# Turning x1 and the experts' rows with 32x32 transposes on VectorE instead of 128x128 products on TensorE

## The reference

```python
x = x + cond_linear(x, cond, w0)            # x1: (4, 1024, 512) fp32, 4096 tokens
# cond_linear: ys = y/sqrt(512); d = rsqrt((ys*ys) @ (w*w) + 1e-8); ((x*ys) @ w) * d
shared = silu(xf @ w1) * (xf @ w3) @ w2     # 512 -> 1024 -> 512, xf = x1 by rows
s = sigmoid(concat([xf, cond]) @ router_W)  # 8 experts; the top 2 of s + bias are used
gates = s_sel / (s_sel.sum + 1e-9)          # combine[token, expert]
h = gelu(einsum('nc,ech->enh', xf, W1e)); y = einsum('enh,ehc->enc', h, W2e)
out = x1 + (shared + sum_e combine * y) / 3 # experts 512 -> 512 -> 512
```

## Time and profile before

| | before |
|---|---|
| time, median of 3 runs | 1152.32 us (1144.98 to 1153.76) |
| the profiled execution's own time | 1147.5 us |
| its span | 1145.7 us |
| PE busy | 1115.5 us, 97% of the span |
| PEld, DVE, ACT, POOL busy | 923.1, 416.6, 334.3, 252.1 us |
| DMA | 218.19 MB, mean 190 GB/s |
| granted TensorE clock | 0.995 of full speed |

### The profile page before, as it was taken

One profiled execution on the slowest core, in us unless ns is written; L12 is line 12 of the kernel. 1 busy time (PEld: TensorE's weight loads), 2 busy tenths in 40 slices (PEclk: granted clock), 3 DMA queues, 4 the chain that ended last, 5 costly groups with the idle time before them and its releaser, 6 DMA issues.

```text
span 1145.7 us, 15826 instructions
## 1 busy us (share of the span) xinstructions
PE 1115.5 (97%) x5260; PEld 923.1 (81%) x5261; DVE 416.6 (36%) x654; ACT 334.3 (29%) x552; POOL 252.1 (22%) x285
## 2 busy tenths in 40 slices
PE   7999999999999999999999989999998899999996
PEld 6888888888888888888887878888887788888884
DVE  6554345657332242323222133333332233333332
ACT  4443533232312122222111123333332222333321
POOL 0000000001121545556620001222211222222222
PEclk9999999999999999999999999999999999999999
DMA  4666867666746897887683088645487854454442
GB/s 168 234 246 255 302 248 257 213 244 240 250 146 230 274 303 276 296 289 223 183 220 110 5 291 284 154 83 98 84 260 250 270 88 85 82 101 81 74 80 40
DMA packets 74141, 218.19 MB, mean 190 GB/s; under 512 B 16176, under 2 KB 17328, under 8 KB 62832
## 3 DMA queue, kind: packets, MB, share of 16 engines
q1 hardware_dynamic: 38240, 133.83, 33.4%
q0 software_dynamic: 21856, 56.72, 22.2%
q10 hardware_dynamic: 14016, 27.27, 7.3%
HBM read 119.40 MB, written 98.65 MB: 190 GB/s over the span
## 4 chain that ended last, share of the span: by engine, by line
PE 59%; DMA 29%; POOL 4%; issue 3%; DVE 2%; SPq 1%; ACT 1%; POOLq 0%; ACTq 0%; DVEq 0%
DMA xs_d<-xrow,sadr 13%; PE banks L489 10%; PE banks L491 10%; PE banks L490 10%; DMA xs_d<-xrow,padr 7%; DMA we<-we_d 5%; PE banks L418 3%; PE banks L417 3%; PE banks L416 3%; PE banks L392 3%; PE banks L379 3%; PE banks L381 3%; PE banks L380 3%; PE banks L475 2%; PE banks L482 2%
## 5 line engine op out<-in xcount | busy, mean ns | idle before, releaser
L1085 POOL DMA_INDIRECT out<-ys,slot x71 | 110.2, 1552 | 448.2 <-DMA out<-ys,slot 266.9
L416 PE MATMUL banks<-xh,w13h 128*128 128x512 f32 x512 | 199.5, 390 | 0.9 <-issue 0.9
L417 PE MATMUL banks<-xl,w13h 128*128 128x512 f32 x512 | 199.2, 389 | 0.0
L418 PE MATMUL banks<-xh,w13l 128*128 128x512 f32 x512 | 199.2, 389 | 0.0
L781 DVE TENSOR_TENSOR gm<-sil,banks 128x512 f32<-128x512 f32 x64 | 43.9, 686 | 273.3 <-ACT sil L603 273.3
L603 ACT ACTIVATE sil<-banks 128x512 f32<-128x512 f32 x64 | 38.2, 597 | 336.8 <-PE banks L418 336.8
L489 PE MATMUL banks<-we,hidth 128*128 x284 | 118.9, 419 | 7.3 <-SPq L312 4.1
L489 PE MATMUL banks<-we,xgth 128*128 x284 | 119.0, 419 | 3.6 <-issue 3.3
L416 PEld LDWEIGHTS banks<-xh,w13h 128*128 128x128 f32 x512 | 96.1, 188 | 21.2 <-issue 1.1
L1002 DVE TENSOR_TENSOR xgtl<-banks,xgth 128x512 fp32r<-128x512 f32 x71 | 49.0, 691 | 174.7 <-ACT xgth L665 174.7
L417 PEld LDWEIGHTS banks<-xl,w13h 128*128 128x128 f32 x512 | 96.1, 188 | 19.9
(11 more groups left out here) (156 smaller groups left out, 1582.3 us busy)
## 6 DMA issues: line engine op xcount, KB each, us to landing
we_d<-ehl SPq DMA_DIRECT2D x32, 1024.0 KB, 4.8
we<-we_d SPq DMA_DIRECT2D x16, 2048.0 KB, 9.0
xg<-xs_d ACTq DMA_DIRECT2D x36, 512.0 KB, 4.4
eraw<-expert_w SPq DMA_DIRECT2D x32, 512.0 KB, 4.4
xrow<-x_d POOLq DMA_DIRECT2D x64, 256.0 KB, 3.4
xin<-xT SPq DMA_DIRECT2D x8, 1024.0 KB, 6.6
x1t_d<-x1t SPq DMA_DIRECT2D x8, 1024.0 KB, 8.7
x_d<-x1tok ACTq DMA_DIRECT2D x8, 1024.0 KB, 8.9
```

The source lines that it names most:

```text
L416: pe.matmul(ps[hc % 2][:, :], w_hi, xh[:, j, c, :], start=(c == 0), stop=False)
L417: pe.matmul(ps[hc % 2][:, :], w_hi, xl[:, j, c, :], start=False, stop=False)
L418: last = pe.matmul(ps[hc % 2][:, :], w_lo, xh[:, j, c, :], start=False, stop=(c == DC - 1))
L1085: pool.indirect_dma_start(out[:, :], IO(slot[:, t, 0:1], 0), ys[:, t % RING, :], None, compute_op=ALU.add).then_inc(added, 16)
```

## The change

- by_token and `idrw` go. `logits(n)` makes 16 fp32 products a block in its place: the stationary side is 32 columns of router weights (`rwide`), the moving side a 128x128 piece of x1t, and the four token pieces s write to partitions 32s to 32s + 31 of `log_ps`. VectorE turns the logits at the end by two 128x512 transposes.
- VectorE turns x1 itself, by 32x32 blocks: four transposes a block (`turn_x1`), from `xin` in the shared stage, steps 4 and 5 of the block before (block 0 after its own step 0). SP stores the result in four transfers of 32 partitions with runs of 512 bytes (`store_x1`, after step 5), into an `x1_d` whose columns are in another order and whose 128-row tiles hold tokens in another order (`token_ids`). `x1tok` shares memory with `outst`, so turns and outputs wait for each other's stores.
- POOL no longer waits for all of x1: `load_row` waits block by block on `x1_out`. It loads each tile once (32 loads) and scatters it twice, in pairs of tiles; ScalarE's waits before block 7 stay. SP's wait for the scatters and the load of `slot` are moved behind the stores and loads of blocks 5 to 7.
- transpose_x goes. The sorted rows come in by four transfers of 32 partitions with 512-byte runs (`load_rows`) for each pair of tiles, and VectorE turns them by one transpose a tile (`turn_x`).
- The factor 1/3 moves from `output` into `product`.

```diff
-        x1tok = sb("x1tok", [2, SUB, D], FP32, 160)
+        xgt = sb("xgt", [2, DC, P], FP32, 192)
+        x1tok = sb("x1tok", [BLK // Q, DC, Q], FP32, 168)
...
+            def store_x1(n):
+
+                sp.wait_ge(x1_turned, DC * (n + 1))
+                for g in range(P // Q):
+                    sp.dma_start(x1_d[n * BLK:(n + 1) * BLK, g * P:(g + 1) * P].rearrange("(a t) d -> t a d", t=Q),
+                                 x1tok[g * Q:(g + 1) * Q].rearrange("p a c n -> p a (c n)")).then_inc(x1_out, 16)
...
             for n in (NBLK - 2, NBLK - 1):
                 store_out(n - 1)
                 load_res(n)
+                if n < NBLK - 1:
+                    store_x1(n + 1)
             weight_loaded(0)
+            sp.wait_ge(pad_out, 16 * 2 * E)
+            for b in range(XB):
+                sp.wait_ge(xrow_out[b], 16 * (K * NT // XB))
+            sp.dma_start(slot[:, :, :], xs_rec).then_inc(slots_in, 16)
...
-                for s in range(SUB):
-                    pe.wait_ge(x1_done, 4 * n + s + 1)
-                    for o in range(DC):
-                        last = pe.matmul(tok_ps[s % 2][:, o // 2, o % 2 * (P + E):(o % 2 + 1) * (P + E)],
-                                         x1t[:, j, o, s * P:(s + 1) * P], idrw[:, o, :], start=True, stop=True)
-                    last.then_inc(tok_done, 1)
+            def logits(n, j):
+
+                for o in range(DC):
+                    pe.wait_ge(x1t_done, 4 * n + o + 1 + 2)
+                    for s in range(SUB):
+                        last = pe.matmul(log_ps[s * Q:(s + 1) * Q, n // 4, n % 4 * P:(n % 4 + 1) * P], rwide[:, o * E:o * E + Q],
+                                         x1t[:, j, o, s * P:(s + 1) * P], start=(o == 0), stop=(o == DC - 1))
+                last.then_inc(log_done, 1)
...
                 for k in range(1, RING + 1):
                     t = RING * i + k
                     matmul1(t, k)
-                    transpose_x(t + 1, k + 1, i + (k + 1) // RING)
                     matmul2(t - 1, k - 1)
                     transpose_h(t, k)
...
-                act.dma_start(xg[:, k % RING:k % RING + PAIR, :],
-                              xs_d[bass.ds(t * P, PAIR * P), 0:D].rearrange("(t p) d -> p t d", p=P)).then_inc(xg_in[j], 16)
+                for g in range(P // Q):
+                    act.dma_start(xg[g * Q:(g + 1) * Q, k % RING:k % RING + PAIR].rearrange("p t a n -> p (t a) n"),
+                                  xs_d[bass.ds(t * P, PAIR * P), g * P:(g + 1) * P].rearrange("(a r) d -> r a d", r=Q)).then_inc(xg_in[j], 16)
...
+            def turn_x1(n, j, c):
+
+                if c == 0:
+                    if isinstance(n, int) and n < 2:
+                        if n:
+                            dve.wait_ge(x1_out, 16 * (P // Q) * n)
+                    else:
+                        dve.wait_ge(out_stored, 16 * (n - 1))
+                dve.transpose(x1tok[:, :, c, :], xin[:, j, c, :].rearrange("p (a t) -> p a t", t=Q)).then_inc(x1_turned, 1)
...
+                if more and hc in (4, 5):
+                    turn_x1(n + 1, (j + 1) % 2, 2 * hc - 8)
+                    turn_x1(n + 1, (j + 1) % 2, 2 * hc - 7)
...
+            def turn_x(t, k, turn):
+
+                if k % PAIR == 0:
+                    dve.wait_ge(xg_in[k // PAIR % 2], 16 * (P // Q) * (turn + 1))
+                dve.transpose(xgt[:, k % 2].rearrange("p c (a r) -> p a c r", r=Q),
+                              xg[:, k % RING].rearrange("p a (c n) -> p a c n", n=Q)).then_inc(xturn_done, 1)
...
+            def load_row(i):
+
+                n, a = i // SUB, i % SUB
+                if a == 0:
+                    pool.wait_ge(x1_out, 16 * (P // Q) * (n + 1))
+                pool.dma_start(xrow[:, i % XB, 0:D],
+                               x1_d[n * BLK:(n + 1) * BLK, :].rearrange("(s a t) d -> a s t d", a=SUB, t=Q)[a]).then_inc(xrow_in[i % XB], 16)
...
+            for i in range(0, NT, 2):
+                for k in range(K):
+                    put_row(i, k)
+                    put_row(i + 1, k)
+                for m in (i, i + 1):
+                    if m + XB < NT:
+                        row_free(m)
+                        load_row(m + XB)
```

More of the change, by code:

```diff
@@ L35 @@
 PADROWS = P
+Q = 32
 ROW = D + 2
@@ L188, in shared_moe_kernel @@
         tok_done = sem("tok_done")
-        x1_done = sem("x1_done")
+        log_done = sem("log_done")
         x1t_out = [sem(f"x1t_out{j}") for j in range(2)]
-        x1_out = [sem(f"x1_out{j}") for j in range(2)]
+        x1_turned, x1_out = sem("x1_turned"), sem("x1_out")
         w_high, w_split = sem("w_high"), sem("w_split")
@@ L468, in _ @@
                     shared_block(2 * h + j, j)
-            def transpose_x(t, k, turn):
-                if k % PAIR == 0:
-                    pe.wait_ge(xg_in[k // PAIR % 2], 16 * turn + 16)
-                pe.wait_ge(xgt_done, t + 1)
-                for c in range(DC):
-                    last = pe.transpose(xt_ps[k % 2][:, c * P:(c + 1) * P], xg[:, k % RING, c * P:(c + 1) * P], ident)
-                last.then_inc(tx_done, 1)
             def transpose_h(t, k):
@@ L955, in _ @@
                 block_step(0, hc, 0, True)
+                if hc == 0:
+                    for c in range(DC):
+                        turn_x1(0, 0, c)
                 if hc in (0, 2, 4):
@@ L1063, in _ @@
             pool.dma_start(xrow[:, XB - 1, D:ROW].bitcast(INT32), padslots[:, 0:2]).then_inc(zero_in, 16)
-            for q in range(XB - 1):
-                load_row(q)
+            for i in range(XB - 1):
+                load_row(i)
             pool.wait_ge(zero_in, 32)
```

126 lines of the change are left out of this document (54 added, 72 removed).

## The result

| | before | after |
|---|---|---|
| time, median (runs) | 1154.3 us (20) | 1159.89 us (20), 1148.28 to 1171.11 |
| ratio to the kernel before, 95% interval | | 1.0062 (1.0032 to 1.0092) |
| the profiled execution's own time | 1147.5 us | 1156.24 us |
| its span | 1145.7 us | 1154.4 us |
| granted TensorE clock | 0.995 | 0.977 |

What follows compares the result with a forecast made beforehand. PE was taken to bound the shared stage, POOL's chain of adding scatters the experts' stage up to scatter 57. 1147.5 - 17 + 20 + 1 = 1151.5, plus 4.8 for the median: 1156 us, range 1138 to 1178.

Steps and rivals of the forecast that it cites:

- Logits, -17 us: Linear stage to up(0,0): narrow products run side by side, 1.3 us a group, less two x1t waits of 2.2 us; -17 us.
- VectorE's turns, 0: Shared stage: VectorE's 32 turns of x1, 22 us of work, hide beside PE and cost nothing.
- x1's store and the scatters, +20: Around block 7: x1's late store delays POOL's last scatters, ScalarE waits, PE stalls; +20 us (+16 to +30).
- it would reach this load some 35 us before x1 is there: POOL's chain reaches its load of tile 28 early and waits some 35 us for block 7 of x1.
- L: Time from a scatter's issue to its landing in POOL's chain to xs_d: 3.2 us (2.8 to 4.5).
- 5.0 + 2L: POOL's time for a pair of tiles scattered to xs_d in two waves, before it loads the next.
- Experts' stage, +1: PE saves 31 us in 71 tiles, but POOL's scatter chain is the bound; +1 us (-18 to +29).
- the +9 for 512-byte runs: Experts' stage: short-run row loads slow 56 quiet scatters by 0.16 us each, to 5.9 us; +9 us.
- Serial products: Rival: the narrow logits products run one after the other, -3 in place of -17; 1170 us, chance 0.25.
- Slower scatters: Rival: 512-byte runs make the experts' stage scatters 6.3 us or more, +22; 1178 us, chance 0.12.
- The faster case: Rival: scatters less disturbed, 5.4 us each, about -20, 1136 us; or block 7's stall goes; chance 0.2.
- The 5.4 for an undisturbed scatter: Experts' stage: the last scatter, 3.81 + 1.55 us, read as the time of a scatter without loads beside it.

Runs made afterwards that it cites:

- experiment 4: Changed kernel with the two loops of the logits exchanged, so four products in a row write to the same 32 partitions: 1172.45 us, ratio 1.0162.
- f1: Changed kernel, but POOL's loads bring 128 neighbouring rows of x1_d instead of four stretches of 32 rows: 1150.42 us, ratio 0.9977.
- f3: Changed kernel with the 64 loads and the load and scatter order of the kernel before, loading 128 neighbouring rows: 1146.69 us, ratio 0.9925.
- f2: Changed kernel, but x1 is stored in four transfers of 128 partitions with 2048-byte runs instead of 32 partitions with 512-byte runs: 1150.79 us, ratio 0.9972.
- e2: Changed kernel with every second adding scatter to the output replaced by a small direct store: 1134.55 us, ratio 0.9817.
- b1: Kernel before, doing only the first of PE's four transposes of each tile of sorted rows: 1158.0 us, ratio 1.0024.
- e3: Changed kernel, each pair of tiles of sorted rows loaded by one transfer of 128 partitions with 2048-byte runs: 1166.4 us, ratio 1.0108.
- b3: b1 with sorted rows loaded as the change does, four transfers with 512-byte runs for each pair of tiles: 1141.08 us, ratio 0.9937.
- experiment 7: The pair b1 and b3: kernel before with fewer PE transposes, with long and with short load runs; 1158.0 and 1141.08 us.

## Why the prediction was right in the time, and where its steps were wrong

- **Logits, -17 us: right, measured -14.3.** The group of block 0 starts at 39.30 us and the next product of linear at 40.31: 1.01 us, less than the 1.3 taken. The two waits for x1t are there with 2.30 us each, as charged (2 x 2.2). Up(0,0) starts 3.85 us after the last groups begin, not 2.6, since it waits 1.90 us for VectorE's split of w13, which the old groups had covered. Some 3 us more went into a later start (the first group begins 0.85 us later than before), small waits and slower records behind them. By the 2.38 that the Trainium skill gives for three packed tiles (TensorE: Matmul & The Clock Gate, section Part 3) a group would take 1.15 us, an estimate; measured is 1.0. Its rule that products in distinct column groups run side by side agrees with experiment 4.
- **VectorE's turns, 0: right.** Two take 1.30 us, and no wait of PE is put down to them.
- **x1's store and the scatters, +20: right place, wrong cause, and 11 short.** 26.7 us of longer wait, 2.9 of two small ones (1.95 for gl, 0.98 for outst) and 1.4 of restart. The step that failed is "it would reach this load some 35 us before x1 is there". It took L, 3.2 us, from two puts at a quiet place of the kernel before, whose own median over all 64 was 4.0, and carried it over, without asking whether the new loads and stores change it. In the changed kernel the median was 5.8. By the prediction's own formula a pair of tiles costs 5.0 + 2L: 11.4 us with 3.2, 16.6 with 5.8. The 13 pairs before the load of tile 28 took 16.5 us each (365.29 to 579.93), and so the chain came to it when x1 was there. Runs f1 and f3 showed that most of the change in L is the form of the loads, f2 that the form of the stores adds to it. The rest of the chain stood: from the load on 31 us forecast, 33.8 measured (30.1 in f1), ScalarE's issues and the path to PE within 0.4 us.
- **Experts' stage, +1: wrong by 9, within its range.** That most of PE's 31 us would not arrive is confirmed by e2 and b1. The last 13 scatters shrank from 81.60 to 75.14 us, -6.5 (forecast -7), though POOL had caught up with PE at scatter 64 and did not lag to the end. The term that failed is the +9 for 512-byte runs: the first 57 scatters took 374.89 us against 376.45. In them the quiet scatters took 5.60 us each and not 5.9, -6 us against the 5.74 of before, and the two stretches beside weight loads 4.5 us more. In the nine traces of this stage the first 57 took 371 to 384 us, so no cost of 9 us shows, and one of a few us could hide in that spread. By the rule of the Trainium skill (DMA: Bandwidth & Descriptors, section Specifications) that 512 bytes still go at line rate, the stage would be 8 us shorter, as the prediction worked out; this trace has -8.0, which agrees, though the nine have -1 to -11.
- **The rivals.** Serial products fell by the group's 1.0 us and experiment 4. Slower scatters fell by the 5.60 us of the changed kernel, and e3 and b3 point the same way. The faster case, "less disturbed than now, because four small loads spread over 2 us", has the sign that e3 and b3 show, but its 5.4 us was not reached, and experiment 7 leaves its cause open. The 5.4 for an undisturbed scatter was a misreading: the wait of 3.81 us in the earlier trace rows was ended by ys, not by the scatter before, so it gives only an upper bound.

The sum missed the profiled time by 4.7 us (1151.5 against 1156.24), out of terms of +11, -9 and +3. It was right to within half a percent because two errors have opposite signs, and that is luck.

## What to carry to other kernels

A latency read beside one traffic holds only for that traffic: read it over the whole stretch in which it will be used, and if a change gives a transfer another shape, count its packets on its queue before carrying over the landing time of what shares the queue. Where an engine waits for a long side chain in program order, look at what stands behind that wait first; moving the wait by six steps was worth 26 us, more than all the work that the change took off PE brought. Work taken off a busy engine arrives only as far as the serial chain beside it has slack, and that is seen not in busy shares but in whether the chain's waits end by its own transfers.

## What the runs showed of the hardware

- A load of 256 KB in four stretches of 32 rows counted 272 packets on POOL's queue, and 80 as 128 neighbouring rows. In the first form scatters beside it landed in 7.1 us, in the second in 5.3 (medians between 400 and 500 us, after and f1). Between 545 and 580 us, with less traffic beside, the first form landed them in 3.9.
- The number of packets alone doesn't rank transfers. With four loads of 128 KB in 512-byte runs on ScalarE's queue in place of one of 512 KB, b3 has four times the packets a load of b1, and its adding scatters took 5.68 us each against 6.10. That long loads make them dear in general is not shown: the kernel before has such loads and 5.66.
- Sixteen fp32 products of 32 by 128 columns take 1.0 us when neighbours write to other groups of 32 partitions, and 2.46 us when four in a row write to the same.
- 32x32 transposes of a 128x512 tile on VectorE take 0.69 us (mean of the 32 of x1) and 0.70 us (mean of the 71 of sorted rows), as long as a tensor operation of that size.
